# Scores and maxima of the first attention as 32-row products of two heads at once, without masked copies of the queries

## What is computed

```python
# x: 4 batches x 256 tokens x 128; ctx: 4 x 512 x 128; H = 16 heads of D = 8
q = layernorm((layernorm(x) @ Wq.T + bq).reshape(B, N, H, D)) * D ** -0.5   # with gamma, beta
k = layernorm((ctx @ Wk.T + bk).reshape(B, M, H, D))                        # with gamma, beta
v = (ctx @ Wv.T + bv).reshape(B, M, H, D)
attn = softmax(einsum('bhnd,bhmd->bhnm', q, k))
out = einsum('bhnm,bhmd->bhnd', attn, v)
x = x + tanh(g_xattn[0]) * (out @ Wproj.T + bproj)
```

## Time and profile before

| what | value |
|---|---|
| median of 3 runs | 864.45 us (863.61 to 864.6) |
| profiled execution: its own time | 863.28 us |
| profiled execution: span | 861.5 us |
| attention 0's quads in the trace | about 44.5 to 185 us |
| PE busy over the span | 747.3 us |
| GpSimd busy in the masked copies (64 of them) | 58.9 us |

### The profile page before, as it was taken

How to read it: one execution, slowest core, us unless ns; L and a number is a source line. 1 busy time by engine, 2 the same in 40 slices (tenths; PEclk the granted TensorE clock), 3 DMA queues, 4 the chain that set the end, 5 groups by cost and what they waited for, 6 DMA issues and landing times.

```text
span 861.5 us, 14142 instructions
## 1 busy us (share of the span) xinstructions
PE 747.3 (87%) x5558; PEld 549.7 (64%) x5558; DVE 560.2 (65%) x1165; ACT 357.5 (41%) x528; POOL 295.4 (34%) x211
## 2 busy tenths in 40 slices
PE   6779999969788988799979999799999566998896
PEld 5656666637577865467656666477676345876784
DVE  5666766627886867686676767677666755365243
ACT  3667676643333364255333553245435330220300
POOL 4365344101011034355533553355555452100100
PEclk9799999988999999799988999799999887999999
DMA  8000000041000030000000000000000000000000
GB/s 174 3 2 2 2 2 2 1 142 56 0 1 1 21 78 1 1 2 1 2 1 1 2 1 2 1 1 2 1 2 1 1 1 2 1 7 0 7 7 6
DMA packets 25553, 11.55 MB, mean 13 GB/s; under 512 B 11832, under 2 KB 24200, under 8 KB 25360
## 3 DMA queue, kind: packets, MB, share of 16 engines
q1 hardware_dynamic: 24480, 10.59, 4.8%
q10 hardware_dynamic: 1008, 0.07, 0.1%
HBM read 10.06 MB, written 0.52 MB: 12 GB/s over the span
## 4 chain that ended last, share of the span: by engine, by line
PE 72%; DVE 18%; issue 5%; ACT 3%; DMA 1%; POOL 0%; SPq 0%; POOLq 0%; DVEq 0%; ACTq 0%
PE ps L1462 69%; DVE o L1271 2%; DVE rs_t L925 2%; PE ps L1473 2%; DVE pmax L1255 2%; ACT v L563 1%; DVE stats L940 1%; DVE rs_y L936 1%; DVE ysum L1372 1%; PE ps L1566 1%; DVE rs_t L918 1%; DMA raw<-in_L_xattn_Wproj_dram 1%; DVE xm L1353 0%; DVE mx L1048 0%; POOL hid_l L557 0%
## 5 line engine op out<-in xcount | busy, mean ns | idle before, releaser
L804 ACT ACTIVATE p<-ps 128x1024 f32<-128x1024 f32 x96 | 96.4, 1025 | 139.9 <-PE ps L1462 139.9
L1462 PE MATMUL ps<-p,v 128*64 128x256 f32 (+1 forms) x1280 | 141.4, 407 | 5.1 <-DVE o L1272 2.3
L1462 PE MATMUL ps<-kqh 64*128 64x256 f32 (+1 forms) x640 | 107.2, 371 | 41.8 <-DVE pmax L1255 32.4
L537 POOL TENSOR_TENSOR acc<-p 128x1024 f32<-128x1024 f32 x32 | 75.7, 2364 | 124.5 <-ACT p L804 124.5
L540 POOL TENSOR_TENSOR acc<-acc,p 128x1024 f32<-128x1024 f32 x32 | 76.2, 2382 | 114.7 <-ACT p L804 114.7
L1462 PEld LDWEIGHTS ps<-p,v 128*64 128x64 f32 (+1 forms) x1280 | 67.6, 132 | 60.2 <-issue 27.3
L1048 DVE TENSOR_REDUCE mx<-ps 128x1 bf16<-128x512 f32 x128 | 82.4, 687 | 36.1 <-PE ps L1462 35.9
L1462 PEld LDWEIGHTS ps<-kqh 64*128 64x128 f32 x640 | 60.5, 196 | 69.1 <-DVE pmax L1255 35.3
L1255 DVE TENSOR_REDUCE pmax<-ps 128x2 f32<-128x1024 f32 x64 | 78.3, 1223 | 28.4 <-PE ps L1462 26.7
L510 POOL TENSOR_SCALAR q<-qst,rmask 128x256 fp32r<-128x256 f32 x64 | 58.9, 939 | 58.6 <-ACT qst L563 58.6
L659 ACT ACTIVATE p<-ps 128x1024 f32<-128x1024 f32 x64 | 65.5, 1026 | 22.3 <-PE ps L1462 20.3
(11 more groups left out here) (254 smaller groups left out, 1496.1 us busy)
## 6 DMA issues: line engine op xcount, KB each, us to landing
w<-in_L_ffn_W_dram SPq DMA_DIRECT2D x1, 2048.0 KB, 12.7
wt<-in_L_ffn_W_dram SPq DMA_DIRECT2D x4, 512.0 KB, 6.1
ctx_all<-in_ctx_dram SPq DMA_DIRECT2D x4, 256.0 KB, 4.7
raw_kv<-in_L_xattn_Wkv_dram SPq DMA_DIRECT2D x1, 1024.0 KB, 4.9
raw<-in_L_ffn_B_dram SPq DMA_DIRECT2D x9, 64.0 KB
xr<-in_x_dram SPq DMA_DIRECT2D x4, 128.0 KB, 3.6
raw_q<-in_L_xattn_Wq_dram SPq DMA_DIRECT2D x1, 512.0 KB, 5.8
wout<-in_L_xattn_Wout_dram SPq DMA_DIRECT2D x1, 512.0 KB, 7.1
```

The source lines that it names most:

```text
L537: pool.tensor_tensor(acc1[:, :], p1[:, s, 0, :], p1[:, s, 1, :], ALU.add).then_inc(g_acc.sem, 1)
L804: act.activation(p1[:, g % 2, u, :], bank(2 * (n % 2), 2), ACT.Exp, scale=SCALE1).then_inc(a_exp1.sem, 1)
L1462: return pe.matmul(o, lhsT, rhs, start=start, stop=stop)
```

## The change

The masked copies, their mask and GpSimd's part are gone. A product takes the 32 partitions of one head from `qst` and `kst` directly, and the maxima's DMA writes row 24 of each of the four strips. Successive products belong to neighbouring strips and write different banks: `row_max0` goes through heads 0, 1, 0, 1, 2, 3, 2, 3, and a group of `scores0` holds two heads and half of the keys, where it held one head and all keys. The numbers of products and their columns stay. `qst` gets 4 slots (it had 2); ACT's copy into it waits for the scores of four quads ago. `onecol` becomes a tile of its own.

```diff
-            def masked0(q):
-                pool.wait_ge(a_qst.sem, q + 1)
-                if q >= SLOTS:
-                    pool.wait_ge(e_st0.sem, e_st0.after(q - SLOTS + 1, 0))
-                for v in range(QUAD):
-                    pool.tensor_scalar(q4[:, q % SLOTS, v, :], qst[:, q % 2, :], rmask[:, v:v + 1], None,
-                                       ALU.mult).then_inc(g_q4.sem, 1)
-
             rest(0)
-            masked0(0)
             rest(1)
             rest(2)
             rest(3)
-            for q in range(1, AQ):
-                masked0(q)
...
             def row_max0(q, n):
                 m = 8 * q + n
-                r, t = divmod(n, 2)
+                r, t = 2 * (n // 4) + n % 2, n // 2 % 2
                 if n == 0:
                     pe.wait_ge(a_kst.sem, q + 1)
-                if t == 0:
-                    pe.wait_ge(g_q4.sem, g_q4.after(q, r + 1))
+                    pe.wait_ge(a_qst.sem, q + 1)
                 if m >= 2:
                     pe.wait_ge(d_max0.sem, m - 1)
-                mm(bank(4 + m % 2), q4[:, q % SLOTS, r, t * P:(t + 1) * P],
-                   kst[:, q % SLOTS, :]).then_inc(e_max0.sem, 1)
+                at = slice(P // QUAD * r, P // QUAD * (r + 1))
+                mm(bank(4 + m % 2), qst[at, q % SLOTS, t * P:(t + 1) * P],
+                   kst[at, q % SLOTS, :]).then_inc(e_max0.sem, 1)
...
-                for k in range(TC):
-                    ins = mm(bank(2 * (n % 2), 2)[:, k * NQ:(k + 1) * NQ], kst[:, q % SLOTS, k * P:(k + 1) * P],
-                             q4[:, q % SLOTS, r, :])
+                for k in range(2):
+                    for j in range(2):
+                        at = slice(P // QUAD * (2 * heads + j), P // QUAD * (2 * heads + j + 1))
+                        ins = mm(bank(2 * (n % 2) + j)[:, k * NQ:(k + 1) * NQ],
+                                 kst[at, q % SLOTS, (2 * chunks + k) * P:(2 * chunks + k + 1) * P],
+                                 qst[at, q % SLOTS, :])
```

More of the change, by code:

```diff
@@ L87, in flamingo @@
         blk16 = sb("blk16", [P, H])
-        rmask = sb("rmask", [P, QUAD])
+        onecol = sb("onecol", [P, 1])
         identb = sb("identb", [P, P], BF16)
@@ L142, in flamingo @@
         kst = area.take("kst", [P, SLOTS, NC_], F32R)
-        qst = area.take("qst", [P, 2, NQ], F32R)
-        q4 = area.take("q4", [P, SLOTS, QUAD, NQ], F32R)
+        qst = area.take("qst", [P, SLOTS, NQ], F32R)
         v0 = area.take("v0", [P, B, TC, V0C])
@@ L230, in flamingo @@
         Q_BANK = (7, 0, 6) + (6,) * (AQ - 3)
-        onecol = ident[:, MAXROW:MAXROW + 1]
         HEAD_BANK = [7] + [6] * (B - 1)
@@ L249, in flamingo @@
         e_kst, a_kst = signal("e_kst"), signal("a_kst")
-        e_qst, a_qst, g_q4 = signal("e_qst"), signal("a_qst"), signal("g_q4", 4)
+        e_qst, a_qst = signal("e_qst"), signal("a_qst")
         e_rbk, e_rbq, d_knk, d_knq = (signal(n) for n in ("e_rbk", "e_rbq", "d_knk", "d_knq"))
@@ L432, in maxima_row @@
                 sp.wait_ge(a_rows0.sem, q + 1)
-                sp.dma_start(q4[MAXROW:MAXROW + 1, q % SLOTS, :, :].bitcast(F32), mrow0[:, q % 2, :]).then_inc(s_mrow.sem, 16)
+                sp.dma_start(qst[MAXROW:P:P // QUAD, q % SLOTS, :].bitcast(F32), mrow0[:, q % 2, :]).then_inc(s_mrow.sem, 16)
             for q in range(AQ):
@@ L672, in stack_q @@
                 act.wait_ge(e_qst.sem, q + 1)
-                if q >= 2:
-                    act.wait_ge(g_q4.sem, g_q4.after(q - 1, 0))
-                copy(qst[:, q % 2, :], bank(Q_BANK[q])[:, 0:NQ]).then_inc(a_qst.sem, 1)
+                if q >= SLOTS:
+                    act.wait_ge(e_st0.sem, e_st0.after(q - SLOTS + 1, 0))
+                copy(qst[:, q % SLOTS, :], bank(Q_BANK[q])[:, 0:NQ]).then_inc(a_qst.sem, 1)
             def stack_k(q):
@@ L680, in stack_k @@
                     act.wait_ge(e_st0.sem, e_st0.after(q - SLOTS + 1, 0))
-                ident_of(kst[:, q % SLOTS, :], bank(K_BANK[q]), onecol).then_inc(a_kst.sem, 1)
+                ident_of(kst[:, q % SLOTS, :], bank(K_BANK[q]), onecol[:, :]).then_inc(a_kst.sem, 1)
             stack_q(0)
@@ L1029, in _ @@
             dve.wait_ge(g_const.sem, 4)
-            dve.tensor_reduce(rmask[:, :], ident[:, :].rearrange("p (r c) -> p r c", r=QUAD), AX,
-                              ALU.add).then_inc(d_cols.sem, 1)
+            dve.tensor_reduce(onecol[:, :], ident[:, MAXROW:P:P // QUAD], AX, ALU.add).then_inc(d_cols.sem, 1)
             norm_x(1)
@@ L1047, in row_max0 @@
                     dve.wait_ge(e_rows0.sem, q - 1)
-                dve.tensor_reduce(mx0[:, q % 2, n % 2, n // 2:n // 2 + 1], bank(4 + m % 2), AX,
+                dve.tensor_reduce(mx0[:, q % 2, n // 2 % 2, 2 * (n // 4) + n % 2:2 * (n // 4) + n % 2 + 1], bank(4 + m % 2), AX,
                                   ALU.max).then_inc(d_max0.sem, 1)
@@ L1612, in scores0 @@
             def scores0(n):
-                q, r = divmod(n, QUAD)
-                if r == 0:
+                q, u = divmod(n, QUAD)
+                chunks, heads = divmod(u, 2)
+                if u == 0:
                     pe.wait_ge(s_mrow.sem, s_mrow.after(q, 16))
@@ L1636, in values0 @@
                         ins = mm(bank(7)[32 * r:32 * r + 32, 0:NQ], v0[:, b, k, h * V0W:h * V0W + 32],
-                                 p0[:, (4 * q + r) % PR0, k * NQ:(k + 1) * NQ], k == 0, k == TC - 1)
+                                 p0[:, (4 * q + 2 * (k // 2) + r // 2) % PR0,
+                                    r % 2 * BANK + k % 2 * NQ:r % 2 * BANK + (k % 2 + 1) * NQ], k == 0, k == TC - 1)
                 if hi == TC:
```

## The result

The changed kernel takes 877.86 us (median of 4 runs, 872.1 to 892.5) against 864.03 (862.81 to 864.6) for the kernel before on the same chip: ratio 1.0151, 95% interval 1.0101 to 1.0202. It is slower, where 856.7 was forecast. The profiled execution took 874.57 us.

What follows compares the result with a forecast made beforehand. PE was taken to bound the kernel, with DVE setting 2.24 us of each quad. Gains 6.2 + 0.4 + 1.2 + 1.4 less 1.5 for the collision gave 7.7 us, so 856.7 us, range 851.5 to 863.

Steps and rivals of the forecast that it cites:

- the fifth rival: In attention 0, narrow products let the clock drop; a dozen quads of up to 13 us lose 70 us: 930; chance 0.03.
- I allow 3 us each way: Whole kernel: allowance for a shift moving a low-clock stretch of a few us onto or off PE's work.
- three signs that the prediction gave for being wrong: Two 32-row products starting a whole product apart; a change costing 0.3 or more; DVE's maxima setting quads longer than 7.3.
- The plain quad: Attention 0, nine plain quads: 7.05 us instead of 7.74, 0.69 won each, 6.2 us together.
- `rows0` waits for DVE's chain: Start of each quad: 2.24 us from the last maxima to `rows0` belong to DVE, so nothing is won there.
- the rivals of half overlap and of none: 32-row pairs in attention 0 overlap by half only: 861.8, chance 0.13; or not at all: 872.8, chance 0.09.
- The price of a change: PE going between array shapes: 0.09 plus 0.11 for the slow first product, 0.20 together, assumed both ways and for 32 rows.
- The last quads: Last two quads: six score groups on the chain, each with its change 0.43 instead of 0.67, win 1.4 us.
- The collision: Preparation: GpSimd's moved `rest(1)` blocks a DVE instruction, 1.97 us instead of 0.36, costing 1.5 us on the path.
- The first collision: Preparation, already in the kernel before: GpSimd's `rest(0)` makes a DVE instruction of 0.36 last 1.97 us.
- Turning iterations: Iterations 5, 9 and 13: shorter last scores less the loss before win 0.1, 0.1 and 0.2, together 0.4 us.
- The sum for attention 0 without the clock: Gains of 6.2 plain quads, 0.4 turning iterations, 1.2 loop start and 1.4 last quads: 9.2 us.

Runs made afterwards that it cites:

- e13: Kernel before with scores and maxima as 64-row pairs, two masked copies a quad: 864.63 us, ratio 1.0011.
- e12: Products alone on PE, no kernel computed: seven lists, mostly turns between shapes of 32-row fours or pairs, 64-row pairs and full products; 64-row turns reached the upper clock after 3.2 us.
- e6: Changed kernel with quads 0 to 3, 14 and 15 back on 128-row products of masked copies: 865.47 us, ratio 1.0053.
- e1: Changed kernel with one more GpSimd wait, so its second subtraction waits for DVE's chain: 881.65 us, ratio 1.0126.
- e2: Changed kernel with 32-row products in the order of before, one head after another, no two side by side: 967.51 us, ratio 1.1186.
- e3: Only the maxima as 32-row pairs, scores on 128-row masked copies and GpSimd's order as in the kernel before: 876.12 us, ratio 1.0155.
- e7: Changed kernel with three more 128-row products of 512 columns a quad at `stack_k`, from quad 3 on: 887.91 us, ratio 1.0301.
- e14: Kernel before with only the maxima as 64-row pairs, scores on 128 rows: 871.78 us, ratio 1.0102.
- e5: Only the scores as 32-row pairs, maxima on 128-row masked copies and GpSimd's order as in the kernel before: 862.55 us, ratio 1.002.
- e9: Kernel before with three tiny 32-row products of 32 columns added a quad, so six more changes of shape: 878.44 us, ratio 1.0193.
- e15: Kernel before with scores and maxima of quads 4 to 15 as 64-row pairs, quads 0 to 3 on 128 rows: 858.49 us, ratio 0.996.
- e16: As e15, but the scores of quads 0 to 3 are 64-row pairs too, only their maxima on 128 rows: 858.36 us, ratio 0.9929 against before.
- e10: Changed kernel with quads 0 and 1 back on 128-row products of masked copies: 873.46 us, ratio 1.0127.
- e11: Kernel before with 32-row pairs for the scores of quads 14 and 15 only: 862.48 us, ratio 1.0017.
- e8: Products alone on PE, without waits: seven lists of whole quads and of turns between shapes; quads of before reached the upper clock after 3.4 us, the changed kernel's after 9.1.
- e4: Products alone on PE: seven lists of full, 64-row, 32-row, mixed and values products, each after a pause; full products reached the upper clock after 3.7 us.

## Why the prediction was wrong

**What failed** is the fifth rival, "the clock falls in attention 0", at 0.03, and with it the sentence "I allow 3 us each way" for the clock. The sum held the clock at nothing within these 3 us; it took some 12.5 to 14.6. The reason against it was that "the 64-row stage, in the earlier trace rows, runs at the starts of the high level". That is true of attention 1 and says nothing of 32 rows, nor of the first quads, where 64-row pairs had the early stretch as well (e13, 30.7 us). Of 32 rows: in e12 the same turns had the upper level after 3.2 us with 64-row pairs and in 31.6 us never with 32-row pairs; in the kernel, e13 has no fall from 81.4 to 170, e6 has three between 100 and 128. The rival's price was off as well. It let a dozen quads run low at up to 13 us each, 930; the changed kernel is low for 47.8 us, not for all, and a quad almost wholly at the lower level takes 10.6 (in e1, from 113.45 to 124.04, with the lower level from 114.5). With one product at a time (e2) nearly all quads are low, at 967.5. None of the three signs that the prediction gave for being wrong came up (products a whole length apart, changes of 0.3 or more, quads over 7.3 at the upper level): none of them was about the clock.

The Trainium skill ("TensorE: Matmul & The Clock Gate", HAM oscillation — how this bites in real kernels) names idle gaps of PE as what brings the clock down. The trace agrees for the fall at 53.05 at most: ahead of it PE was busy 4.62 of 6.85 us. It does not agree for what follows: from 65 to 80 PE is busy 14.64 of 15.00 us at 0.50, and e1 falls at 114.5 after 3.4 us without idle time and is then busy 17.00 of 17.00.

**What the runs show of the cause.** That the lower clock is the term that failed is shown. What in the narrow products brings it is shown in part; in the traces there are two conditions. The early stretch (near 50 to 80) comes where the maxima of the first quads are narrow, of 32 rows (after, e1, e2, e3, e7) or of 64 (e13, e14), and not where they are on 128 rows (before, e5, e6, e9, e15, e16). In e10, where they are narrow from quad 2 on, a stretch begins at 63.0. What differs is how long it lasts more than the fall itself: before and e16 fall there too, but have the upper level again after 3.4 us, and e9 has two such pieces. e16 shows that 64-row scores make no difference; for 32-row scores e5's trace says the same, though two of its executions may not. The later falls between the first and the last quads come where scores and maxima are both 32-row pairs (after, e1, e6, e7, e10), not with 64-row pairs (e13, e15, e16) nor with one of the two narrow (e3, e5). In the last quads e13 has one too (170.1 to 176.9), and the mean clocks of e11 and e15 leave more of them open. That the collision brings the stretch (e1) fell, and so did that changes of shape alone do it in this kernel (e9); in bare lists of products, turns of two kept the lower level whatever the rows (e8, e12). Why the narrow maxima matter most in the first quads was not separated from the preparation that runs between them, and e7 shows that more full-width work is no cure; both stay open.

**By the forecast's own steps:**

- The plain quad: 7.17 instead of 7.05, a gain of 0.59 for 0.69. From `rows0` to the values it is 1.73 (90.89 to 92.62), forecast 1.72; in the second half the scores, maxima and values take 1.86 (92.62 to 94.48) where 1.76 was forecast. Of that, scores to second maximum are 0.45 (93.62 to 94.07; forecast 0.44), and second maximum to values 0.41 (forecast 0.32), and there the 0.1 is.
- `rows0` waits for DVE's chain, 2.23 for 2.24: right. Pairs side by side and 0.43 for scores with a change: right, so the rivals of half overlap and of none fell.
- The price of a change, taken from 64-row rows, was a little high for 32: 0.32 for a tiny product with two changes (e9), so 0.16 at most for each, where the forecast has 0.20 with what is slow behind it.
- The last quads: 1.4 forecast, 1.2 measured (e11).
- The collision: an instruction of 1.97 in place of 0.36 forecast, 1.92 measured; right in place and size. The first collision is still there (1.99). The 1.5 that it was to cost on the path is 0.4 to 1.1 at the first maximum by e2 and e7 against e11, e13 and e16.
- Turning iterations: 9.41 where 9.28 was before; 0.1 lost, not 0.1 to 0.2 won each.
- The sum for attention 0 without the clock: from the first maximum to the end e16 wins 6.2 (its narrow maxima only begin with quad 4), where the forecast's terms for all quads are 9.2, and 8.3 with the measured quad. By these numbers the terms of PE were 1 to 3 us too high together; the term left out, some 12.5 to 14.6, is larger than the whole sum.

## What to carry to other kernels

Before making products of a busy TensorE narrower, price the lower clock as a term, not as a remote rival: PE time saved in a stretch is worth nothing if a third of the work there is lost. Read the granted clock by stretch first in the changed profile, and take evidence from rows of the same number of partitions. Where two heads fit in halves of the array, 64-row pairs gave the same PE time as 32-row pairs here (7.17 a quad) and kept the clock far better, with half of the masked copies of before outside the first quads; leave the first quads' maxima wide. Look at the mean clock of every execution, not only of the one that was traced: four of e15's ten lost part of the gain.

## What was not expected of the hardware

- At the lower level PE is not idle at all (e4: 26.27 busy of 26.30 us) and stayed there through lists of single 32-row products, of pairs on two fixed strips (25.6 us) and of short turns between shapes (57.6 us, with 32-row pairs; 43.1 with 64-row pairs). 32-row pairs over changing strips had the upper level after 6.8 us, but there products of more than two strips ran beside each other, half as many again per us.
- One changed kernel on one chip spread over 872.1 to 892.5 us, with 0.921 to 0.887 of mean clock, where the kernel before stays within 2 us on that chip; e16 stays within 2 us too. On two other chips the kernel before itself spread over some 12 us (853.77 to 865.34 with e5, 854.41 to 866.61 with e9), so a small ratio needs many runs.
- A change of shape costs 0.16 us with its share of a tiny product (e9). Narrow maxima alone, with their changes, gave no gain: a quad takes 7.87 in e3, 7.75 before.
